# A graph network's two layers on one core: hardware loops written out as straight code

## The reference

```python
# layer 0: u sums, for each of 8 edge types r, the mean of neighbours' rows times weight[r]
out = x @ root + bias
for r in range(8):
    mask = (edge_type == r)
    sums = segment_sum(x[src] * mask[:, None], dst, n)
    cnt  = segment_sum(mask, dst, n)
    out += (sums / maximum(cnt, 1)[:, None]) @ weight[r]
u = out
z = concatenate([u, x], axis=1) @ w_gate + b_gate
x = layernorm(x + tanh(u) * z + x * (1 - z))
# layer 1: graph convolution with self loops, norm = dinv[src] * dinv[dst]
h = x @ W
x = layernorm(x + relu(segment_sum(h[src] * norm[:, None], dst, n) + b))
```

## Time and profile before

| | us |
|---|---|
| median of the runs | 1878.89 |
| all runs | 1865.23, 1878.89, 1885.79 |
| span of the profiled execution | 1849.0 |

### The profile page before, as it was taken

One profiled execution on the slowest core, in us unless ns is written; L12 is line 12 of the kernel. 1 busy time (PEld: TensorE's weight loads), 2 busy tenths in 40 slices (PEclk: granted clock), 3 DMA queues, 4 the chain that ended last, 5 costly groups with the idle time before them and its releaser, 6 DMA issues.

```text
span 1849.0 us, 27446 instructions
## 1 busy us (share of the span) xinstructions
PE 1688.9 (91%) x7621; PEld 1362.7 (74%) x7621; DVE 1053.6 (57%) x1938; ACT 564.8 (31%) x923; POOL 877.0 (47%) x879
## 2 busy tenths in 40 slices
PE   7999999608988999999989999999999889999997
PEld 6888888506766777788778888777877667777786
DVE  4446210015655766477667762787687875455386
ACT  3221111102332333255444542455355331111000
POOL 0018777767777750366556531676466421121000
PEclk9999999958999999999989999999999889999999
DMA  6322333300212122657656634676576642442743
GB/s 218 112 80 59 93 99 94 87 10 24 86 35 75 51 75 86 234 175 229 188 170 206 181 117 158 181 238 188 185 219 181 212 152 91 147 145 78 285 141 111
DMA packets 115112, 254.09 MB, mean 137 GB/s; under 512 B 25062, under 2 KB 25437, under 8 KB 114871
## 3 DMA queue, kind: packets, MB, share of 16 engines
q0 software_dynamic: 39904, 89.23, 17.6%
q1 hardware_dynamic: 41142, 92.41, 14.7%
q10 hardware_dynamic: 33952, 71.20, 10.3%
HBM read 185.13 MB, written 77.80 MB: 142 GB/s over the span
## 4 chain that ended last, share of the span: by engine, by line
PE 51%; issue 18%; DVE 4%; POOL 2%; DVEq 1%; another core or an unknown queue 1%; DMA 1%; ACT 0%; POOLq 0%; ACTq 0%; SPq 0%
PE PG L704 38%; PE PM L728 8%; PE PM L715 3%; PE PG L793 1%; POOL GATE L649 1%; POOL WORK L645 1%; DVE WORK L1243 1%; DVE SPLO L1236 1%; DVEq L1220 1%; DMA XROWS<-in_x_dram 0%; DVE ONEHOT L1232 0%; DVE WORK L1205 0%; POOL records L546 0%; DVE WORK L1226 0%
## 5 line engine op out<-in xcount | busy, mean ns | idle before, releaser
L704 PE MATMUL PG<-WHI,XHI 128*128 128x512 f32 x1600 | 639.7, 400 | 70.0 <-DVE WLO L1081 70.0
L704 PE MATMUL PG<-WHI,XLO 128*128 128x512 f32 x1600 | 628.5, 393 | 0.0
L704 PE MATMUL PG<-WLO,XHI 128*128 128x512 f32 x1600 | 628.5, 393 | 0.0
L704 PEld LDWEIGHTS PG<-WHI,XHI 128*128 128x128 f32 x1600 | 303.9, 190 | 135.5 <-issue 66.1
L704 PEld LDWEIGHTS PG<-WHI,XLO 128*128 128x128 f32 x1600 | 303.0, 189 | 64.5
L704 PEld LDWEIGHTS PG<-WLO,XHI 128*128 128x128 f32 x1600 | 303.7, 190 | 61.2
L621 POOL DMA_INDIRECT WORK<-y,IDX x176 | 188.1, 1069 | 144.9 <-DVE SPLO L1236 78.5
L1081 DVE TENSOR_TENSOR WLO<-WRAW,WHI 128x512 fp32r<-128x512 f32 x176 | 122.5, 706 | 230.9 <-ACT WHI L885 201.7
L892 ACT ACTIVATE STAGE<-PG 128x512 f32<-128x512 f32 x200 | 118.9, 595 | 412.0 <-PE PG L704 391.9
L546 POOL DMA_INDIRECT records<-RREC,IDX x160 | 204.5, 1278 | 61.1 <-issue 43.4
L621 POOL DMA_INDIRECT RAW<-y,IDX x176 | 189.6, 1078 | 91.6 <-DVE SPLO L1236 49.8
(11 more groups left out here) (169 smaller groups left out, 1915.8 us busy)
## 6 DMA issues: line engine op xcount, KB each, us to landing
y<-STAGE ACTq DMA_DIRECT2D x200, 256.0 KB
WRAW<-in_L_gnn_weight_dram SPq DMA_DIRECT2D x30, 1024.0 KB
WRAW<-in_L_gnn_w_gate_dram SPq DMA_DIRECT2D x8, 1024.0 KB
WORK<-y SPq DMA_DIRECT2D x10, 512.0 KB, 5.6
GATE<-y SPq DMA_DIRECT2D x10, 512.0 KB
x<-X ACTq DMA_DIRECT2D x10, 512.0 KB, 6.0
WORK<-x SPq DMA_DIRECT2D x10, 512.0 KB, 4.7
WORK<-in_x_dram SPq DMA_DIRECT2D x9, 512.0 KB, 4.4
```

Source lines behind the costliest of these rows:

```text
L704: last = pe.matmul(PG[:, bank, :], lhs[:, k, t * P:(t + 1) * P], rhs[:, j % 2, k, :], start=(k == 0 and n == 0), stop=(k == KT - 1 and n = ...
```

## The change

Every hardware loop but the branch in the convolution (a data-dependent one, L854) becomes a Python loop, which writes its body out once a turn with constants in place of registers. The order of the work on each engine is the same. Only the value that picks a pair's group still comes through a register. Line numbers behind the changed `Chain` fall by about ten.

```diff
@@ one_each, and the same in dense @@
     body, s0 = at
-    with eng.Fori(body, body + 2) as i:
+    for i in range(body, body + 2):
         for n in range(SUBSTEPS):
             step(i, s0 + n, [((i - body) * SUBSTEPS + n, n)])
...
@@ Chain @@
     def link(self, ins):
         ins.then_inc(self.sem, 1)
         self.at = self.at + 1
-        self.steps += 1
         self.eng.wait_ge(self.sem, self.at)
...
@@ gpsimd: scatter; the weights' and gathers' loops alike @@
-            with pool.Fori(1, turns) as i:
+            for i in range(1, turns):
                 for b in range(2):
                     scatter_half(i, b, False)
...
@@ gate stage: tensor; the other engines alike @@
-            with pe.Fori(1, NT - 2) as i:
+            for i in range(1, NT - 2):
                 gate(i + 1)
...
@@ gate stage: vector @@
-            X1_STEPS = 4
...
-            with dve.Fori(0, NT - 3) as i:
-                chain.enter(i, X1_STEPS)
+            for i in range(0, NT - 3):
                 u_low(i + 2)
                 make_x1(i + 1)
                 h_low(i, HST_HI[:, :], HST_LO[:, :])
                 x1_low(i + 1)
                 make_u(i + 3)
-            chain.leave(NT - 3, X1_STEPS)
...
@@ convolution: tensor; the other engines alike @@
-            with pe.Fori(1, NT // 2) as i:
+            for i in range(1, NT // 2):
                 for b in range(2):
                     conv(2 * i + b, b, False)
```

More of the change, by code:

```diff
@@ L421, in _ @@
             for h in range(2):
-                with sp.Fori(1 - h, R // 2) as i:
+                for i in range(1 - h, R // 2):
                     for b in range(2):
@@ L591, in _ @@
                 weight_half(0, b, True)
-            with pool.Fori(1, turns_w) as i:
+            for i in range(1, turns_w):
                 for b in range(2):
@@ L660, in _ @@
             add_root(2)
-            with pool.Fori(0, NT - 3) as i:
+            for i in range(0, NT - 3):
                 add_gate(i + 1)
@@ L667, in _ @@
                 rstd(t)
-            with pool.Fori(NT, 2 * NT) as t:
+            for t in range(NT, 2 * NT):
                 rstd(t)
@@ L1038, in _ @@
             tile_body(0, True)
-            with act.Fori(1, NT - 2) as i:
+            for i in range(1, NT - 2):
                 tile_body(i, True)
@@ L1052, in store @@
                     act.dma_start(out[d * P:N, :], result[b][0:rows, :]).then_inc(out_done[b], 16)
-            with act.Fori(0, NT // 2 - 1) as i:
+            for i in range(0, NT // 2 - 1):
                 for b in range(2):
@@ L1454, in _ @@
             two_tiles(0)
-            with dve.Fori(1, NT // 2 - 1) as i:
-                chain.enter(i - 1, 6)
+            for i in range(1, NT // 2 - 1):
                 two_tiles(i)
-            chain.leave(NT // 2 - 2, 6)
             finish(NT - 1, 1)
```

4 lines of the change are left out of this document (1 added, 3 removed).

## The result

The changed kernel took 1811.97 us (median of 5 runs, 1797.81 to 1818.12), against 1878.89 us for the kernel before in the same comparison: ratio 0.966, 95% interval 0.961 to 0.971. Forecast were 1855.5 us and a range of 1832 to 1876. The sign was right; the gain was 67 us where 23 were forecast.

What follows compares the result with a forecast made beforehand. TensorE was taken to bound most of it, GpSimd's scatter until about 403 us, and late loop messages elsewhere; -19.0 - 2 - 1 - 1.3 = -23.3 us gave a 1825.7 us span, about 1855.5 us median, range 1832 to 1876.

Steps and rivals of the forecast that it cites:

- the two returns: VectorE's late jumps back in the counting and first message loops (5.80, 7.70 us); stall and lower clock together, -19.0 us.
- VectorE's register work: Address and wait-value work in pair loops, 0.14 us a pair: -2 us in the second message loop, -1 us in counting.
- the gate stage: Loops over tiles: VectorE's chain 0.18 us shorter in each of seven tiles, -1.3 us; bounds 0 and 12.4 us.
- the 29.9 us of offset: Median run time above the profiled execution's span, added unchanged to the forecast span; held uncertain by some 10 us.
- Rival A: The 5.80 and 7.70 us gaps are not the jump's and stay; only -4.3 us, about 1875 us; chance 0.16.
- Third return: VectorE's long jump back at line 99, idle 10.50 us, hides because ScalarE's weight half released what follows; term 0.
- Other engines' returns: Jumps back of TensorE, ScalarE and SyncE, costed at nothing because TensorE's queue of matmuls covers them.
- Scatter and added code: GpSimd's register work in the scatter already lies under its issues, and added code costs TensorE nothing: terms 0.
- Rival B: GpSimd's straight code comes late in the scatter and second message loop: slower, about 1890 us; chance 0.10.
- Rival C: Gate stage's normalisation falls from 2.84 to 0.81 us, 14.5 us more, plus 11.5 us dense waits: about 1830 us; chance 0.12.
- the collision: In the gate stage GpSimd's add starts 0.07 us before VectorE's normalisation, which takes 2.84 us; the forecast had the order stay.

Runs made afterwards that it cites:

- late occasion: Chip or occasion where semaphore events from TensorE reach waiting engines late: kernel before 1878.89 to 1882.77 us, changed kernel 1811.97 to 1818.28 us.
- calm chip: Chip or occasion where semaphore events from TensorE come on time: kernel before 1825.01 to 1826.33 us, changed kernel 1792.88 us, ratio 0.981.
- first comparison: Changed kernel, all loops but the convolution's branch straight, first timed against the kernel before: 1811.97 against 1878.89 us, ratio 0.966.
- exchanging the two calls: Changed kernel with GpSimd's add of the bias moved ahead of the reciprocal root in the gate loop: 1777.72 us and 1806.39 us.
- thrice-loaded group: Changed kernel with each pair's group loaded into VectorE's register three times instead of once: 1797.74 us, 1838.91 us and 1849.89 us.

## Why the prediction was right in its mechanism and wrong in its size

In short: the large term, the two returns, was right. Two terms were mis-sized, VectorE's register work (-3 us put down; the code it belongs to was worth 36 us more on a late occasion than on a calm one) and the gate stage (-1.3 put down, 9.4 measured, most of it clock), and the 29.9 us of offset, carried over unchanged, was no constant.

*The two returns, -19.0:* right. On the calm chip the two stretches that hold them went from 141.4 to 133.1 and from 155.7 to 146.7 us, 17.3 together; in the first comparison's traces it was 7.6 and 10.2. The matched stretches of equal length gave a good price for stall and clock at once. Rival A is out: with VectorE straight the gap is gone, and with the other engines' pair loops straight, or every loop but the pair and gate loops, it stays. The compare-and-branch figure of "Advanced Engine Details and Errata", section Control Flow Timing, in the Trainium skill does not hold for VectorE's jumps here: twelve on the path, in six traces, took 5.75 to 7.70 us each.

*Third return, -0:* right within what can be seen; dense body 2 is the same with and without it (153.3 and 153.4 us). Other engines' returns were costed at nothing because TensorE's queue would cover them; the number was right for another reason, since their jumps are short (ScalarE's 0.24 to 0.33 us). Writing out their loops was worth 4 us on a calm chip and 9 on a late one when VectorE kept its own, and nothing that can be told on top of VectorE's.

*Register work, -2 and -1:* right where notices are on time (dense body 1 0.7 us, counting turn 1 -0.3, within what two traces differ by). Wrong where they are late, as in the first comparison: VectorE's straight pair code was worth 36 us more on a late occasion than on a calm one (56 less 20). In the first comparison's traces that shows in counting turn 1 (12 us) and the dense bodies (14 us, with TensorE's waits for the low half down from 13.5 us to 2.3), stretches without a return on the path. My upper bounds for the two terms, 12 and 11 us, made 23 at most, so the range failed here, not only the choice within it. It was narrower than its own terms allow, besides: the bounds written down add up to 19 + 12 + 11 + 12.4 = 54 us, and the range of the gain stopped at 30. I had the sign of it in front of me and passed it over: runs 20 us apart and a profiled execution faster than all of them, which I booked as an offset that the change leaves alone. An offset that differs from run to run can be lost time with a cause, and a change can save some of it.

*Gate stage, -1.3:* this step failed too, and not because of the chip. Its mechanism was right: VectorE's chain shrank and TensorE's wait fell from about 2.22 to 1.98 us a tile, 1.7 us in seven. But the clock was not costed. The forecast took stall and clock together at the returns, from matched stretches, and the stall alone here. It was worth 9.4 us in the first comparison and 11.0 on the calm chip (162.8 less 151.8), 12 to 15 in the medians of the kernel with these loops alone.

*Scatter and added code, 0:* right. The idle time in front of the first weights is unchanged, and all loops outside pair and gate stages are worth some 2 us together. Rival B, slower, never showed: GpSimd's straight code came in time.

*Rival C:* the collision did not turn round, since the order stayed, as the forecast argued. Its price was about right, in part by luck: exchanging the two calls gave 12 to 15 us, where C had put 7 x 2.07 = 14.5, but the waits that went were six, 10.9 us. Its other half, that the dense loop's waits go as well (11.5 us), did come true in the first comparison, against the forecast's -2.

Summed for a calm chip, the terms that the experiments isolate are 21 (pair loops on all engines) + 13 (gate, mean of two) + 2 = 36, against 33.5 for the whole (1826.33 less 1792.88), each with some 4 us of uncertainty. On a late one, 56 (VectorE's pair loops) + 9 (the others') + the gate stage's calm 13 make 78, against 64 by the medians and 61 to 74 by the ratios. Whether parts overlap there can't be told from that.

*Still open:* what makes TensorE's notices late. One chip's number stands on both lists, so it may be the time and not the chip. They come in counting and the dense phase, where VectorE and ScalarE read what TensorE has just written, and not in the gate stage, which does so too. The late traces also lack semaphore events in those phases, and some in the scatter (from 200 to 400 us 2149 to 2247, where calm ones have 2701 to 2757), and lack none in the gate loop. Whether one cause delays the notices and loses the events, and whether recording a run takes part in it, is open: no run here shows the program unrecorded. Why less code on VectorE saves some 35 us of it is argued, not shown: a pair in flight has some slack, and what VectorE does between a late notice and the next one-hot is added to it. That register work, and not the missing jumps, carries it follows from the thrice-loaded group only in kind, since that dose, 1.2 us a pair, is larger than what the change took away. A kernel with register work kept and only the jump gone was not tried.

## What to carry to other kernels

Where TensorE waits for a two-engine ring, price a shorter wait with the clock that it gives back, from stretches of equal length with and without the fall: here 0.25 us of wait was worth 1.9 us a tile. A spread of runs, with a profiled execution that lies below all of them, was here the sign of lost time that came and went; look for waits on events that came late, and count what a tighter ring saves of it. And look at what runs beside a step that is slow in some places and fast in others: exchanging two calls on an idle engine was worth nearly half as much as writing out every loop on a calm chip.

## What the runs showed of the hardware that was not expected

- VectorE's jump back over a long body took 5.75 to 7.70 us (twelve on the path, in six traces) and 5.29 to 5.70 in the dense loop, over 658 to 783 rows; ScalarE's in the same loops, over 259 to 491 rows, took 0.24 to 0.33 us.
- Notices of TensorE come up to 6 us late in some phases, on some occasions, and 0.31 us after the matmul's start on others, for the same program: some 54 us of 1826 for the kernel before. The traces of those occasions lack a third of the semaphore events, in the same phases.
- TensorE's clock halved for a few microseconds behind stalls of 2.21 to 2.25 us in a row of gate tiles, behind three of six of 2.14 to 2.19, and behind none of 1.96 to 2.00. That is what this kernel's rhythm gave, and no more is claimed.
- A register load of VectorE takes its sequencer 0.62 us with what belongs to it; 327 us of such loads added some 5 us to the program on a calm occasion, and 23 to 32 on late ones.
- VectorE's subtract-and-multiply over 1024 columns took 0.81 us alone and 2.84 us beside GpSimd's add over 1024 columns (2.36 us).
